# An attention kernel whose last three steps are written out by hand, with another order of maxima, values and sums

## The reference

```python
Q = _split_heads(x @ Wq.T + bq)
K = _split_heads(x @ Wk.T + bk)
V = _split_heads(x @ Wv.T + bv)
tQ = _split_heads(tokens @ Wq.T + bq)
tK = _split_heads(tokens @ Wk.T + bk)
cQ = Q + tQ
cK = K + tK
scores = jnp.einsum('bhqd,bhkd->bhqk', cQ, cK) / jnp.sqrt(jnp.float32(HEAD_DIM))
attn = jax.nn.softmax(scores, axis=-1)
out = jnp.einsum('bhqk,bhkd->bhqd', attn, V)
...
x = x + out
```

## Time and profile before

| | us |
|---|---|
| median of 3 runs | 687.12 (686.11 to 687.62) |
| the profiled execution | 690.45 |
| its span | 688.7 |
| mean granted PE clock over the span | 0.978 |

### The profile page before, as it was taken

One profiled execution on the slowest core, in us unless ns is written; L12 is line 12 of the kernel. 1 busy time (PEld: TensorE's weight loads), 2 busy tenths in 40 slices (PEclk: granted clock), 3 DMA queues, 4 the chain that ended last, 5 costly groups with the idle time before them and its releaser, 6 DMA issues.

```text
span 688.7 us, 10047 instructions
## 1 busy us (share of the span) xinstructions
PE 667.9 (97%) x3528; PEld 451.3 (66%) x3528; DVE 541.5 (79%) x818; ACT 375.3 (54%) x659; POOL 490.5 (71%) x205
## 2 busy tenths in 40 slices
PE   6899999999999999999999999999999999999986
PEld 4677766666776666677666666776666677665421
DVE  4386788888888888888888888888888888888736
ACT  6325655555565555565555565555555556556452
POOL 5506777788777778877777887777778776667780
PEclk9899999999999999999999999999999999999787
DMA  7924345553434555343455543434554333444111
GB/s 230 244 53 102 88 115 138 139 135 98 116 100 109 138 138 140 101 115 100 102 138 140 138 115 102 110 94 136 139 139 122 82 101 93 113 124 124 32 48 46
DMA packets 48274, 79.85 MB, mean 116 GB/s; under 512 B 9824, under 2 KB 9824, under 8 KB 48224
## 3 DMA queue, kind: packets, MB, share of 16 engines
q1 hardware_dynamic: 48224, 79.21, 43.2%
HBM read 19.95 MB, written 8.39 MB: 41 GB/s over the span
## 4 chain that ended last, share of the span: by engine, by line
PE 89%; DVE 3%; DMA 2%; issue 2%; SPq 1%; POOL 1%; POOLq 1%; ACT 1%; DVEq 0%; ACTq 0%
PE bank L193 24%; PE bank L262 18%; PE bank L277 17%; PE bank L292 15%; PE bank L240 13%; DVE mf L520 1%; PE bank L300 1%; DMA Ks<-lo 1%; DMA xr<-xT 1%; DVE part_sums L533 1%; POOL A L670 1%; POOLq L40 1%; DMA Pt<-xT 1%; PE bank L309 1%; SPq L722 1%
## 5 line engine op out<-in xcount | busy, mean ns | idle before, releaser
L439 ACT ACTIVATE Pt<-bank 128x512 f32<-128x512 f32 x512 | 301.2, 598 | 240.1 <-PE bank L277 157.7
L520 DVE TENSOR_REDUCE mf<-bank 128x1 f32<-128x512 f32 x512 | 344.6, 685 | 107.3 <-PE bank L262 106.2
L670 POOL TENSOR_TENSOR A<-A,Pt 128x2048 f32<-128x2048 f32 x62 | 284.4, 4588 | 4.9
L277 PE MATMUL bank<-Qs,Ks 98*128 98x512 f32 x512 | 212.4, 416 | 4.3 <-ACT Pt L439 2.5
L262 PE MATMUL bank<-Ks,Qs 96*128 96x512 f32 x512 | 210.1, 410 | 4.2 <-DVE mf L520 2.4
L670 POOL TENSOR_TENSOR A<-Pt 128x2048 f32<-128x2048 f32 x31 | 142.6, 4600 | 4.0 <-DVE part_sums L533 4.0
L277 PEld LDWEIGHTS bank<-Qs,Ks 98*128 98x128 f32 x512 | 97.6, 191 | 69.6 <-ACT Pt L439 46.1
L652 POOL TENSOR_TENSOR Xl<-xr,Xh 128x512 fp32r<-128x512 f32 x28 | 36.0, 1288 | 121.2 <-ACT Xh L407 121.2
L262 PEld LDWEIGHTS bank<-Ks,Qs 96*128 96x128 f32 x512 | 98.3, 192 | 31.4 <-DVE mf L520 6.2
L292 PE MATMUL bank<-Pt,V 128*32 128x512 f32 x992 | 115.4, 606 | 0.0
L193 PE MATMUL bank<-Xh,Wh 128*128 128x512 f32 x256 | 101.8, 398 | 0.8 <-DVE Wl L489 0.8
(11 more groups left out here) (52 smaller groups left out, 325.5 us busy)
## 6 DMA issues: line engine op xcount, KB each, us to landing
Qs<-hi SPq DMA_DIRECT2D x64, 256.0 KB, 3.6
Ks<-hi SPq DMA_DIRECT2D x64, 256.0 KB, 3.6
Qs<-lo SPq DMA_DIRECT2D x32, 256.0 KB, 4.1
Ks<-lo SPq DMA_DIRECT2D x32, 256.0 KB, 4.0
res<-xT SPq DMA_DIRECT2D x32, 256.0 KB, 2.9
outT<-ot SPq DMA_DIRECT2D x32, 256.0 KB, 3.5
xr<-xT SPq DMA_DIRECT2D x28, 256.0 KB, 2.7
Qs<-mt SPq DMA_DIRECT2D x128, 4.0 KB
```

The costliest lines, as they stand in the source:

```text
L277: e.matmul(STB[u % 2][:, :], Ks[0:98, sl, j, kc * P:(kc + 1) * P], Qs[0:98, sl, j, :], start=True, stop=True).then_inc(t_st, 1)
L439: e.activation(Pt[:, kc, j, :], STB[u % 2][:, :], ACT.Exp, scale=SCALE).then_inc(a_e, 1)
L520: e.reduce_max(mf[:, g % 2, 4 * j + qc:4 * j + qc + 1], MXB[u % 2][:, :], AXX).then_inc(v_mx, 1)
L670: e.tensor_tensor(A[:, :, :], Pt[:, 0, :, :] if kc == 1 else A[:, :, :], Pt[:, kc, :, :], ALU.add).then_inc(p_a, 1)
```

## The change

Steps 0 to 28 stay as they are. The last three steps are written out:

- **Step 29**: the 23 maxima that are left go two to a slot (TAIL_MAXIMA), the last in slot 12. values(29), chunks 0 and 1, follow slot 12. The order of DVE is: finish group 27, the maxima, and only then key_sums(28).
- **Score banks**: from step 30 on the scores use four banks, the two of the projections too (`st_bank`), so score u waits for exponential u-4.
- **Values** come in halves: chunks 0 and 1 of a group in slot 11 (slot 12 in step 29) of its own step, chunks 2 and 3 in slot 3 of the next; of group 31 the chunks 2 and 3 stand apart at the end.
- **Totals** of 28 in slot 3 of step 30 and of 29 in slot 3 of step 31.
- **Sums** of the groups 30 and 31: DVE adds chunks 0 and 1 (`add_first`), PE multiplies this and the chunks 2 and 3 by ones (`last_sums`, three times four matmuls). POOL adds nothing for these groups; its last work is add(29, 3). The sum of group 29 goes to V[:, 0] instead of A, that of group 31 too.
- **Residuals** of the groups 30 and 31 are loaded early, into hi and xr, and the last output has a place of its own.

```diff
+TAIL_MAXIMA = (1, 1, 2, 2, 2, 2, 2, 2, 2, 2, 2, 2, 1, 0, 0, 0)
+EARLY_AT, LATE_AT, LAST_SUMS_AT = 11, 3, 6
...
+        def st_bank(u):
+            return (STB + RB)[u % 4] if u >= SLOTS * (G - 2) else STB[u % 2]
...
+        def added_up(g):
+            return V[:, 0, :, :] if g in (G - 3, G - 1) else A
...
+            def last_sums(g, bk, kc):
+                if kc is None:
+                    e.wait_ge(v_a, g - (G - 2) + 1)
+                else:
+                    e.wait_ge(a_e, st_unit(g, kc, 3))
                 for j in range(4):
+                    m = e.matmul(bk[32 * j:32 * j + 32, :], ones[:, :],
+                                 added_up(g)[:, j, :] if kc is None else Pt[:, kc, j, :],
+                                 start=(kc is None), stop=(kc == KC - 1))
...
+            for n in range(SLOTS):
+                scores(G - 2, n)
+                if n == LATE_AT:
+                    values(G - 3, (2, 3))
+                    e.wait_ge(v_mx, SLOTS * G)
+                    totals(G - 4, MXB[0])
+                if n == EARLY_AT:
+                    values(G - 2, (0, 1))
+
+            for n in range(SLOTS):
+                scores(G - 1, n)
+                if n == LATE_AT:
+                    values(G - 2, (2, 3))
+                    e.wait_ge(v_f, finished(G - 4, 1))
+                    totals(G - 3, MXB[0])
+                if n == LAST_SUMS_AT:
+                    for kc in (None, 2, 3):
+                        last_sums(G - 2, MXB[1], kc)
+                if n == EARLY_AT:
+                    values(G - 1, (0, 1))
+            values(G - 1, (2,))
+            e.wait_ge(v_f, finished(G - 3, 1))
+            for kc in (None, 2, 3):
+                last_sums(G - 1, MXB[0], kc)
+            values(G - 1, (3,))
...
+            add(G - 4, 3)
+            parts(G - 2)
+            add(G - 3, 1)
+            parts(G - 1)
+            add(G - 3, 2)
+            add(G - 3, 3)
```

More of the change, by code:

```diff
@@ L285, in values @@
                     e.wait_ge(v_tb, 6)
-                for kc in range(KC):
+                for kc in chunks:
                     if c == 0:
@@ L301, in totals @@
                 m.then_inc(t_l, 1)
[L303 to L306, removed]
+            def last_sums(g, bk, kc):
[3 more added lines that the diff above has]
+                    e.wait_ge(a_e, st_unit(g, kc, 3))
                 for j in range(4):
-                    h = H - 4 + j
-                    m = e.matmul(OB[1][32 * j:32 * j + 32, :], V[:, (B - 1) % 2, kc, h * HD:(h + 1) * HD],
-                                 Pt[:, kc, j, :], start=(kc == 0), stop=(kc == KC - 1))
+                    m = e.matmul(bk[32 * j:32 * j + 32, :], ones[:, :],
+                                 added_up(g)[:, j, :] if kc is None else Pt[:, kc, j, :],
+                                 start=(kc is None), stop=(kc == KC - 1))
                 if kc == KC - 1:
[L312 to L322, removed]
+                    m.then_inc(t_l, 1)
             condition(0, 0)
@@ L358, in tensor_program @@
                 project(k, g, n)
-            for t in range(G):
-                work = [(k, t + 3, n) for k in "vqk" if t + 3 < G for n in range(12)]
+            for t in range(G - 3):
+                work = [(k, t + 3, n) for k in "vqk" for n in range(12)]
                 done = 0
@@ L365, in tensor_program @@
                     u = SLOTS * (t + 1) + n + MAX_LEAD
[L366 to L368 removed]
+                    maxima(u, t - 2 if n == VALUES_AT + 1 and t >= 2 else None)
                     for k, g, i in work[done:done + PROJ[n]]:
@@ L373, in tensor_program @@
                         if t >= 2:
-                            e.wait_ge(v_mx, min(u, SLOTS * G))
+                            e.wait_ge(v_mx, u)
                             totals(t - 2, MXB[(u + 1) % 2])
[L376 to L385, removed]
+                        values(t - 1, range(KC))
+            u = SLOTS * (G - 2) + MAX_LEAD
+            for n in range(SLOTS):
+                scores(G - 3, n)
+                for i in range(TAIL_MAXIMA[n]):
+                    maxima(u, G - 5 if n == VALUES_AT + 1 and i == 0 else None)
+                    u += 1
+                if n == VALUES_AT:
+                    e.wait_ge(v_mx, u - 1)
+                    totals(G - 5, MXB[u % 2])
+                    values(G - 4, range(KC))
+                if n == EARLY_AT + 1:
+                    values(G - 3, (0, 1))
+            for n in range(SLOTS):
[6 more added lines that the diff above has]
+                    values(G - 2, (0, 1))
+            for n in range(SLOTS):
+                scores(G - 1, n)
[13 more added lines that the diff above has]
+            values(G - 1, (3,))
         def scalar_program(e):
@@ L776, in sync_program @@
             stack(1, 2)
-            for t in range(G):
+            for t in range(G - 2):
                 b, kc = divmod(t + 3, KC)
@@ L788, in sync_program @@
                     store(t - 2)
-                if t + 1 < G:
-                    maxima_rows(t + 1)
-            for g in (G - 2, G - 1):
-                load_res(g)
+                maxima_rows(t + 1)
+            load_res(G - 4)
+            maxima_rows(G - 1)
+            load_res(G - 2)
+            load_res(G - 1)
+            store(G - 4)
+            load_res(G - 3)
+            for g in (G - 3, G - 2, G - 1):
                 store(g)
```

148 lines of the change are left out of this document (91 added, 57 removed).

## The result

The changed kernel takes 682.8 us (median of 20 runs, 681.76 to 687.6) against 686.82 of before (20 runs, 685.88 to 689.08): a ratio of 0.9946, 95% interval 0.9933 to 0.9959, so 0.54% less, where 1.2% was forecast. The difference of the medians is 4.0 us, and 682.8 stands at the upper edge of the range that was forecast. The profiled execution took 681.76, its span is 680.0.

The account below looks back on a forecast made before the run. PE bound the middle; the end waited on DVE, POOL and K rows. The scheduled span ended at 680.0 against 688.7, 8.7 less; 0.5 for hand-overs left 8.2, so 687.12 - 8.2 = 678.9 us, range 676.5 to 682.8.

Parts of the forecast that it names:

- set the pace: Steps 30 and 31: ACT's exponentials were to set the pace, at 0.59 us each.
- the tight place, bank 0: Step 30: bank 0 free at 656.3 after finishing group 28, against a need at 656.5; called the tightest place.
- Maxima: Step 29: maxima two to a slot; eleven at half clock take 7.8 us, the last reduced at 646.2 instead of 655.1.
- took the fall as it was: Step 29: the clock was assumed to fall as before, full to 637.3 and then half.
- the prediction's third rival: Step 29: the clock stays full, eleven maxima take 7.3, the first half 1.8; 1.7 us earlier, 677.2; chance 0.12.
- near 646: Sign in step 29: the last reduction of a maximum ends near 646 if right, past 650 if the pair loop costs more.
- near 674: Sign at the end: DVE's last chain starts near 674.
- ACT's gaps at every half: Sign in steps 30 and 31: ACT runs many exponentials together, with gaps under 1 us at slots 3 and 6 alone.
- the difference is what carries over: The sum's last step: the profiled execution was 3.3 us above the median, so 8.2 was taken off 687.12, giving 678.9.
- the clock falls in the gaps: Rival, new step 30: each clock fall between halves of values costs 1.7 us; two falls give 682.3; chance 0.22.
- The clock does not fall in step 29: The same rival as the prediction's third rival: 1.7 us earlier, 677.2; chance 0.12.

Follow-up runs that it names:

- max1: The changed kernel with maxima one to a slot again (16 in step 29, seven in step 30) and totals(28) in slot 7: 681.96 us, ratio 0.9904 to before.
- fill29: The changed kernel with one unread 128-row product after each maximum of step 29 from slot 3 on (19 products): 679.08 us, ratio 0.9867 to before.
- pool30: The changed kernel with group 30's sums made as before (three POOL adds, key_sums, totals): 686.73 us, ratio 1.0005 to before.
- max4: The changed kernel with four banks for the maxima of step 29 from slot 3 on: 678.52 us, ratio 0.986 to before; again 678.04 us, 0.9858.

## Why the prediction missed by half

**The direction and most of the new steps 30 and 31 were right.** Forecast from the end of the first half of values to the last chain: 674.3 - 648.4 = 25.9. Measured: 674.2 - 647.1 = 27.1. ACT's pitch was not 0.59 but 4.03 / 8 = 0.50, and its stops were 1.0 to 2.0 instead of 0.35 to 1.6; the two cancel as far as exponential 4 of step 31, which starts 15.8 us after that first half and was forecast at 15.65. The 1.2 arise behind it, where PE's row has no pause from 662.3 to the last sums: there PE's work set the time, and not ACT, which the schedule had "set the pace". The last chain took 5.8 (5.7 forecast). POOL ended at 655.1 (656.0 forecast), and the tight place, bank 0, held: group 28 was finished at 654.9, values(30) began at 655.39.

**The step that failed is the one named "Maxima".** "Eleven maxima take 5.5 x 1.43 = 7.8", the last at 646.2, 19.0 after values(28). It took 21.0. Two things were missed. The first maximum of group 31 now comes before its K rows have landed: 0.88 us for Ks<-lo, a wait that the old step 29 did not have. It is not the pairs that bring it, since one to a slot waits 0.80 as well (max1); in the old order key_sums(28) stood among DVE's maxima and held PE up for longer (0.97 us, at 635.34), so the likely cause is that they were moved away. I had looked past SP's queue at that place. The old row:

```profile
635.34 0.50 PE L262 MATMUL bank<-Ks,Qs 96*128 96x512 f32 x1 [0.97 <-DVE mf L520]
```

And I "took the fall as it was", at 10.1 us after values(28) began; it came at 8.0 (632.3), and three matmuls at half clock then took 1.58 and not 1.43, since the second maximum of a pair waits for DVE and the score behind it for that.

fill29 measures the clock's share: with nearly the same wait for Ks<-lo (0.76) but full clock the end is 53.1 instead of 55.7. That 53.1 is near the schedule's 52.8 means nothing, since the schedule counted a half clock in; with a full one it gives 52.8 - 1.7 = 51.1 by the prediction's third rival. The 2.0 above that are 0.8 at the first ten maxima (done 11.75 us after values(28) began, 10.97 forecast), which is the wait, and the 1.2 of the last steps. So the 2.9 that the changed kernel's end is longer than forecast are about 0.9 of half clock beyond the 1.7 that was counted, 0.8 of the wait and 1.2 of steps 30 and 31. The first half of values was 1.6 later by the first two (it took 2.6 and not 3.0), the last chain 2.8 by all three.

The signs that the prediction gave did not show this. The last maximum was reduced at 645.3 ("near 646"), POOL ended at 655.1 and the last chain began at 674.2 ("near 674"), because values(28), and with it all that follows, began 2.9 us earlier in this profile than in the one of before. Only ACT's gaps at every half, 1.0 us and more, were a sign that failed.

**The second is the sum's last step**, "the difference is what carries over". It was made against one execution, whose end was 1.6 us longer than that of the next profile of the same kernel, with the clock down for 10.2 us in step 29 instead of 6.8. Of 8.2, 2.4 went to the schedule (2.9, of which 0.5 was allowed for) and 1.6 to this base; what is left, 4.2, is about the 4.0 of the medians.

**The rivals.** The first, "the clock falls in the gaps", gave 682.3, near the measured time, for another reason: in both profiles of the changed kernel the clock was full from 645.9 or 646.6 to the end of PE's work, and it fell in step 29, where I had it fall myself. That this rival's number came so near is luck. The gaps between halves may matter in slower executions: of the 20 runs those at a mean clock of 0.990 took 681.8 to 682.8 and the two at 0.982 took 687.2 and 687.6, but they have no profile. "The clock does not fall in step 29" (677.2) did not happen in the changed kernel; fill29 and the first profile with four banks for the maxima have it, at 679.1 and 678.5. That the change was faster at all rests on three parts together: taking away any of the score banks, the halves or the products with ones takes back 13, 3.8 or 4 us, all or more of the gain, and in each case a part of that is clock; the pairs bring nothing. The prediction's count of the clock in the old end is one short, too: it fell three times, at 637.3, 657.8 and 671.5, and rose at 647.6, 664.6 and 678.3. The rise and the fall that it left out are in these windows of before (the clock is the column ahead of the last two):

```profile
664.00:665.00 1.00, 1.00 (x12) 0.30 (x8) 0.22 (x1) 0.51 (x2) 1.00 (x1) 0.68 0.00 0
671.00:672.00 1.00, 0.21 (x1) 0.00 (x0) 1.00 (x2) 0.92 (x2) 0.00 (x0) 0.73 0.00 0
```

In step 29 the clock was 0.50 for 13.7 us with pairs over two banks and for 3.4 us or not at all with pairs over four; one to a slot over two banks kept it at 1.00 (max1), and before, also one to a slot over two banks, lost it. The section "A second HAM failure mode: psum-queue depth-cycling" of the Trainium skill ("TensorE: Matmul & The Clock Gate") bears on this: a PE that pauses briefly between groups of matmuls while it cycles through banks has its clock go down and up. The runs agree in so far as PE paused briefly ahead of the fall (0.31 and 0.88 us) and lost its clock; that the number of banks alone decides they do not show.

## What to carry to other kernels

Where DVE sets PE's pace and PE is part of the time idle, the price of the next stretch depends on the clock that the idling leaves behind: here two more banks (4.1 us), or even products that nobody reads (3.6 us), were worth as much as the whole new order (4.0 us). Compare ends of profiles from a common event on, give the signs of a forecast from such an event too, and take more than one profile of the kernel before, ahead of subtracting them: its own spread at the end was as large as 40% of the gain. When instructions are moved forward, or a wait ahead of them goes, look up when the data of the first one lands, in the transfer queue's rows.

## What the runs showed of the hardware

- DVE's add of two SBUF tiles (128x2048) takes 2.25 to 2.29 us alone and makes no headway under an add on POOL: 6.01 us where POOL's ended 3.85 after its start (pool30), 4.02 where it ended 1.9 after (max4), 2.69 where it ended 0.5 after (fill29). Less the part under POOL's add, that is 2.2 us each time. DVE's key_sums, with one SBUF input, kept its pace beside POOL (two in 2.33 us at 646.07 in the changed kernel, under an add that ran from 645.85). The Trainium skill, "SBUF — State Buffer", section "SBUF: two separate sides", states this of the port pair that the two engines share: a DVE operation with two SBUF inputs and a GpSimd one exclude each other for a whole instruction. The runs agree. Here it cost nothing with the changed order, where POOL was done at 655.09 and the add began at 655.01.
- A back-to-back maximum costs 0.65 us on DVE from two banks (fill29) and 0.60 from four (max4), an exponential 0.59 on ACT from two and 0.50 from four (4.03 / 8). The time that a single one shows in the rows (0.69 and 0.60) is not what it costs in a queue.
- One product of 128 rows after each of 19 maxima kept the clock at 1.00 through step 29, and PE's extra work made the kernel 3.6 us faster.
